# Edge aggregation of a graph layer: rank masks and running maxima moved into a PSUM bank

## What is computed

```
seg_sum  = segment_sum(edge_attr, src, 12500)
seg_max  = segment_max(edge_attr, src, 12500)        # 0 where a node has no edge
seg_mean = seg_sum / max(count, 1)
h   = relu(concat([seg_sum, seg_max, seg_mean, u]) @ W1 + b1)
out = x + h @ W2 + b2
```

## Time and profile before

| | |
|---|---|
| median of 3 runs | 4669.58 us (4665.87 to 4673.83) |
| the profiled execution | 4668.22 us, its span 4665.3 us |
| TensorE matmul busy | 3045.1 us, 65% of the span |
| VectorE busy | 2912.0 us, 62% |
| ScalarE busy | 1421.9 us, 30% |
| POOL busy | 3441.4 us, 74% |
| mean granted TensorE clock | 0.657 of full speed |

### The profile page before, as it was taken

How to read it: one execution, slowest core, us unless ns; L and a number is a source line. 1 busy time by engine, 2 the same in 40 slices (tenths; PEclk the granted TensorE clock), 3 DMA queues, 4 the chain that set the end, 5 groups by cost and what they waited for, 6 DMA issues and landing times.

```text
span 4665.3 us, 87454 instructions
## 1 busy us (share of the span) xinstructions
PE 3045.1 (65%) x18710; PEld 2270.5 (49%) x18710; DVE 2912.0 (62%) x11699; ACT 1421.9 (30%) x4649; POOL 3441.4 (74%) x3144
## 2 busy tenths in 40 slices
PE   5566667766666666666666777767766776677466
PEld 3455445544444444444444556555645555465345
DVE  6577557754555445555444777777757777577564
ACT  3322332233333333333333222222232222322133
POOL 5777778877777777777777788888877777788700
PEclk9977557855555555555555777777757777587666
DMA  7899863311111111111111333333213222133132
GB/s 288 325 354 338 323 219 103 89 24 25 26 26 25 25 25 25 26 26 25 25 25 50 93 92 92 92 92 92 69 53 85 77 76 76 55 95 108 38 113 77
DMA packets 410043, 454.46 MB, mean 97 GB/s; under 512 B 65002, under 2 KB 381460, under 8 KB 409620
## 3 DMA queue, kind: packets, MB, share of 16 engines
q1 hardware_dynamic: 309876, 401.37, 26.3%
q0 software_dynamic: 100000, 51.40, 4.6%
HBM read 221.50 MB, written 231.02 MB: 97 GB/s over the span
## 4 chain that ended last, share of the span: by engine, by line
POOL 69%; issue 22%; POOLq 3%; DMA 2%; DVE 2%; PE 1%; SPq 1%; ACT 0%; DVEq 0%; ACTq 0%
POOL sorted_rows L435 69%; POOLq L435 2%; DMA win<-sorted_rows 1%; DVE raised L786 1%; DVE raised L778 1%; DMA sorted_rows<-zeros 1%; POOLq L432 1%; DMA sorted_rows<-edges,position 0%; SPq L303 0%; POOLq L427 0%; POOLq L430 0%; PE misc_ps L577 0%; DMA edges<-in_edge_attr 0%; SPq L373 0%; DVE late L875 0%
## 5 line engine op out<-in xcount | busy, mean ns | idle before, releaser
L435 POOL DMA_INDIRECT sorted_rows<-edges,position x3125 | 3419.2, 1094 | 970.6 <-issue 969.6
L495 PE MATMUL place_ps<-start_sb,hot_block_t 98*128 98x128 bf16 x3125 | 889.7, 285 | 1227.5 <-DVE rank_f L719 1226.6
L606 ACT ACTIVATE start_sb<-start_ps 98x128 bf16<-98x128 f32 x3125 | 867.5, 278 | 1738.4 <-PE start_ps L491 844.4
L491 PE MATMUL start_ps<-hot_owner,hot_block 128*98 128x128 bf16 x3125 | 981.2, 314 | 149.5 <-ACT start_sb L606 107.2
L495 PEld LDWEIGHTS place_ps<-start_sb,hot_block_t 98*128 98x128 bf16 x3125 | 372.7, 119 | 1337.4 <-DVE rank_f L719 1317.7
L734 DVE SCALAR_TENSOR_TENSOR position<-rank_c,src_f 128x5 int32<-128x5 f32 x625 | 103.9, 166 | 1438.7 <-DMA sorted_rows<-edges,position 1429.0
L719 DVE CUSTOM_DVE_ANT_0 picked<-place_ps,hot_owner 128x128 bf16<-128x128 f32 x3125 | 885.8, 283 | 87.5 <-issue 72.1
L497 PE MATMUL place_ps<-hot_owner,earlier 128*128 128x128 bf16 x3125 | 898.3, 287 | 0.0
L491 PEld LDWEIGHTS start_ps<-hot_owner,hot_block 128*98 128x98 bf16 x3125 | 461.6, 148 | 627.5 <-ACT start_sb L606 621.7
L522 PE MATMUL misc_ps<-win,ident_f 128*128 128x224 f32 x2548 | 751.8, 462 | 0.0
L468 PE MATMUL same_ps<-hot_block_t 98*128 98x128 bf16 x3125 | 660.7, 290 | 86.0 <-DVE earlier L711 46.5
(11 more groups left out here) (76 smaller groups left out, 1367.1 us busy)
## 6 DMA issues: line engine op xcount, KB each, us to landing
sorted_rows<-zeros SPq DMA_DIRECT2D x110, 1568.0 KB, 25.8
win<-sorted_rows SPq DMA_DIRECT2D x56, 1344.0 KB
edges<-in_edge_attr SPq DMA_DIRECT2D x625, 80.0 KB
sorted_rows<-edges,position POOLq DMA_INDIRECT x3125
win<-sorted_rows SPq DMA_DIRECT2D x28, 1008.0 KB
win<-sorted_rows SPq DMA_DIRECT2D x14, 1680.0 KB
win<-sorted_rows SPq DMA_DIRECT2D x14, 1568.0 KB
win<-sorted_rows SPq DMA_DIRECT2D x14, 896.0 KB
```

Of the source, the lines that this page charges most:

```text
L435: nc.gpsimd.indirect_dma_start(out=rows[:, :], out_offset=bass.IndirectOffsetOnAxis(ap=position[:, t:t + 1], axis=0), in_=edges[:, k, j * ...
L491: nc.tensor.matmul(start_ps[0:BLOCKS, 0:P], hot_block[:, t, :], hot_owner[:, t, :], start=False, stop=False, skip_group_check=True).then_i ...
L495: nc.tensor.matmul(place_slot(j), hot_block_t[:, slot, j * P:(j + 1) * P], start_sb[:, j, :], start=True, stop=False)
L606: nc.scalar.activation(start_sb[:, j, :], start_ps[0:BLOCKS, 0:P], ACT.Copy)\
```

## The change

`peak_ps` is a PSUM bank of its own, 512 fp32 columns: `peak`, 448 columns, holds a running maximum of both halves of a pair, and `beyond`, 64 columns, holds the mask. The bank comes from `place_ps`, which shrinks from three banks to two; `PLACE_BANK` and `PLACE_USER` change accordingly, so tile 0 of a group now waits for the pick of tile 4 of the group before. `raised` has room for both halves, which is found by laying `paired` over `hot_block_t` and `earlier` (`lent`). Since 64 columns hold a mask of at most 9 planes, each half is masked and raised in two parts (`raise_part`). Half 0 is raised in group 0, half 1 in group 1; groups 2 and 3 take the maximum of both halves together, plane by plane, into `peak` (`take_ranks`), and `keep_peak` takes it into `run_max`. The last stage keeps halving `raised` (`take_max`), with the raise in two parts and the mask now behind the wait for the load.

```diff
+        peak_ps = ps("peak_ps", [P, BANK_COLS], FP32)
+        peak = peak_ps[:, 0:2 * COLS].rearrange("p (h n) -> p h n", h=2)
+        beyond = peak_ps[:, 2 * COLS:BANK_COLS]
...
-        PLACE_BANK = [0, 1, 0, 1, 2]
-        PLACE_USER = [3, 3, 2, 2, 5]
+        PLACE_BANK = [0, 1, 0, 1, 0]
+        PLACE_USER = [1, 3, 2, 2, 2]
...
+                def raise_part(s, h, col, r, a, z, steps):
+                    mask = beyond[:, 0:(z - a) * SLOTS].rearrange("p (r b) -> p r b", b=SLOTS)
+                    nc.vector.tensor_tensor(mask, left_t[...], iota_f[...], ALU.is_le).then_inc(unit_step, 1)
+                    dve.wait_ge(unit_step, steps + 1)
+                    return nc.vector.scalar_tensor_tensor(raised[:, h, a:z, :], mask, -FLT_MAX,
+                                                          win[:, h, a:z, :], ALU.mult, ALU.add)
+                def take_ranks(s, steps, a, z):
+                    for r in range(max(a, 1), z):
+                        prior = raised[:, :, 0, :] if r == 1 else peak
+                        if r > 1:
+                            dve.wait_ge(unit_step, steps + (r + 5))
+                        nc.vector.tensor_tensor(peak, raised[:, :, r, :], prior, ALU.max).then_inc(unit_step, 1)
+                def keep_peak(s, col, steps):
+                    dve.wait_ge(unit_step, steps + (depth[s] + 5))
+                    mine = run_max[:, bass.ds(col, 2 * SLOTS), :]
+                    nc.vector.tensor_tensor(mine, mine, peak, ALU.max).then_inc(unit_step, 1)
...
-                        if g in (0, 2):
-                            mark_beyond(of, col, r, steps + h * unit_steps[of])
-                            dve.wait_ge(win_loaded[h], p * 16 + 16)
-                            raise_half(of, h).then_inc(win_raised, 1)
-                        if g in (1, 3):
-                            dve.wait_ge(win_raised, p * 2 + (h + 3))
-                            take_max(of, col, steps + h * unit_steps[of])
+                        if g in (0, 1):
+                            dve.wait_ge(win_loaded[g], p * 16 + 16)
+                            if g == 1:
+                                dve.wait_ge(win_raised, p * 2 + 3)
+                            raise_half(of, g, col + g * SLOTS, r, steps + 3 * g)
+                        if g == 2:
+                            dve.wait_ge(win_raised, p * 2 + 4)
+                            take_ranks(of, steps, 0, half)
+                        if g == 3:
+                            take_ranks(of, steps, half, depth[of])
+                            keep_peak(of, col, steps)
```

More of the change, by code:

```diff
@@ L82, in build @@
     PAIRS = ROUNDS * sum(parts)
-    unit_steps = [2 + len(levels(d)) for d in depth]
-    step_base = [sum(2 * ROUNDS * parts[j] * unit_steps[j] for j in range(s)) for s in range(SEGS + 1)]
+    last_steps = 4 + len(levels(depth[LAST]))
+    pair_steps = [6 + d for d in depth[:LAST]] + [2 * last_steps]
+    step_base = [sum(ROUNDS * parts[j] * pair_steps[j] for j in range(s)) for s in range(SEGS + 1)]
     STEPS = step_base[SEGS]
@@ L774, in mark_beyond @@
                                             ALU.is_le).then_inc(unit_step, 1)
                     dve.wait_ge(unit_step, steps + 1)
-                def raise_half(s, h):
                     return nc.vector.scalar_tensor_tensor(
-                        raised[:, 0:depth[s], :].rearrange("p r (b f) -> p r b f", f=FEAT),
-                        beyond[:, 0:depth[s], :].unsqueeze(3).to_broadcast([P, depth[s], SLOTS, FEAT]), -FLT_MAX,
-                        win[:, h, 0:depth[s], :].rearrange("p r (b f) -> p r b f", f=FEAT), ALU.mult, ALU.add)
@@ L783, in take_max @@
-                def take_max(s, col, steps):
-                    left, done = depth[s], 1
-                    for folded, kept in levels(depth[s]):
-                        nc.vector.tensor_tensor(raised[:, 0:folded, :], raised[:, 0:folded, :],
-                                                raised[:, left - folded:left, :], ALU.max).then_inc(unit_step, 1)
+                        raised[:, h, a:z, :].rearrange("p r (b f) -> p r b f", f=FEAT),
+                        mask.unsqueeze(3).to_broadcast([P, z - a, SLOTS, FEAT]), -FLT_MAX,
```

54 lines of the change are left out of this document (33 added, 21 removed).

## The result

The changed kernel takes **4390.92 us** (median of 4 runs, 4387.55 to 4395.1), the kernel before 4670.3 us in the same comparison (4665.87 to 4673.83): a ratio of 0.9403, 95% interval 0.9386 to 0.9419. Forecast were 4375 us and a range of 4335 to 4465. The profiled execution took 4387.55 us, its span is 4385.8.

The account below looks back on a forecast made before the run. POOL's scatters were taken as the bound, held up by VectorE instructions with two SBUF inputs. 4668.2 - 319 + 12 (lag) + 12 (last stage) = 4373, with 1.4 for the median 4375 us; range 4335 to 4465.

Parts of the forecast that it names:

- Raises and maxima no longer hold POOL: Scatters beside a pair's reduction stop waiting for VectorE instructions with two SBUF inputs: -345.6 us at most, -319 after remaining holds.
- The one-hots: Stream instructions still with two SBUF inputs; hold scatters if VectorE stops waiting: +15 us, bounds 0 and 87.
- VectorE's work per pair: Masks, split raises and maxima in PSUM cost VectorE +1.5 us a pair at depth 12, +1.2 to +2.2 elsewhere.
- two passes in the bank: Rival: PSUM bank read and written in turn, each of 637 maxima 0.47 us dearer; about 4575 us, 5 in 100.
- the running maximum becomes the bound: Rival: the dependent row of maxima through one bank is slow, at 1.5 us each 4810 us; 4 in 100.
- the maxima still hold POOL: Rival: maxima with PSUM as second input still hold scatters, +73 us, 4448 us; 8 in 100.
- does not do what it says: Rival: the mask in PSUM frees nothing and the 345.6 us stay; 4682 us, 3 in 100.
- Both rules that were weighed: Skill rules: PSUM source 65 ns dearer, sum about 4390; raises at half rate from two SBUF inputs, sum 4363.
- What of it reaches POOL: VectorE's lag beyond its 23.6 us lead over POOL's scatters in the stream: +12 us, bounds 2 and 29.
- VectorE falls behind: Rival: maxima and raises each 0.1 us dearer, spill 54 us instead of 2; about 4425 us, 16 in 100.
- The last stage: Masks and a second raise part on the chain after the load: about 1.0 us for ten iterations, +12 us, bounds 5 and 20.
- DMA 0 and the placing banks 0: Neither busy DMA engines beside depth 8 nor fewer placing banks cost time; upper bounds 23 us and 0.3 us a group.

Follow-up runs that it names:

- all_in_sbuf: The changed kernel with the whole new bank, masks and running maximum, in SBUF instead of PSUM; order and split raises kept; 4511.79 us.
- maxima_only: The changed kernel with masks in SBUF and raises whole, as before the change; maxima plane by plane against the PSUM bank stay; 4552.07 us.
- whole_masks: last_as_before, with the stream's running maximum in SBUF, one whole PSUM mask for both halves and one raise a half; 4368.57 us.
- short_sums: The changed kernel with TensorE's sums beside the stream over only the first and last plane, so the result is not whole; 4368.06 us.
- last_as_before: The changed kernel with its last stage as before: one whole mask made before the wait for the load, one raise; 4386.39 us.
- banks_only: The kernel before, with only the placing products moved to two banks; 4674.93 us against 4669.89 in the same comparison.
- one_reduce: The changed kernel with the stream's chain of maxima replaced by one strided tensor_reduce per half; 4465.71 us.

## Why the prediction was right, and which terms were off

The forecast was the likeliest case with its sign and its main mechanism, 16 us short of the median. One of its own signs of being wrong came true all the same: POOL waits 39.9 us for `position`, and it had named 30; nor is POOL's idle time the 0.3 us a scatter that it had expected. By its own steps:

- **Raises and maxima no longer hold POOL:** right. Forecast -345.6 at most and -319 in the sum, measured -335.6. The masks in PSUM hold 0.2 us in all (forecast under 1), the first maxima 4.9 (forecast 56 x 0.155 = 9; with L less 0.17 the same formula gives 4.6). **The one-hots** were given +15, over a cost before that was taken as nothing; it was 15.7 us, and they took 22.3 - 15.7 = +6.6: the phase does wander, but VectorE still waits for POOL in most of the stream.
- **VectorE's work per pair:** right. The half raise is 1558 ns (1.56 forecast), the maximum 628 (0.62), a mask 211 (0.2); a mask written to SBUF takes 203 (all_in_sbuf), so the write to PSUM costs 8 ns. So "two passes in the bank" and "the running maximum becomes the bound" fell with these rows, "the maxima still hold POOL" with maxima_only, and "does not do what it says" with both. Both rules that were weighed are against the rows: 1558 ns for 1344 columns is what they take from two SBUF inputs too (1.56 us in all_in_sbuf). The Trainium skill ("VectorE: DVE Perf Modes", the errata section) had 65 ns more for a PSUM source, and by it the sum was 4390, next to the measured 4390.92; yet the maximum takes 628 ns from PSUM and 626 from SBUF (in whole_masks), so the time came out there by another way.
- **What of it reaches POOL:** the term that failed in size. I took +12, with bounds 2 and 29; measured +51.7. POOL's windows in the changed kernel, 11 chunks of depth 12 and 2 of depth 15 in which it follows VectorE:

```profile
2801.60:3187.40 385.80, 271.61 (x275) 0.79 0.35 103
4035.70:4110.10 74.40, 49.91 (x50) 0.82 0.25 71
```

  That is 35.1 us a chunk (forecast 33.5) and 37.2 (forecast 36.3). The step that failed is "its need is the stretch less its waits on scatters". The pair's own work is not the cause: masks, raises, maxima and the gaps before them take 15.3 us a chunk in these windows and took 13.8 before, the +1.5 of the forecast. Two other things make the 1.6. First, a `position` that no longer waits for a landing still starts 0.18 us behind `rank_c`, 0.90 us a chunk for five, where next to nothing (0.11) was left once the waits for landings were taken off: +0.8. Second, the 25 picks, with the gaps before them, take 6.25 us a chunk and took 5.37: +0.9. That second part is TensorE's: in a stretch of short_sums in which POOL follows VectorE the picks take 5.28 us again, and the 0.90 us stay:

```profile
2933.20:3171.50 238.30, 172.97 (x176) 0.52 0.36 106
```

  These are 7 chunks of 34.0 us, 1.0 less than in the changed kernel, and that at a lower clock. POOL's own chunk is 25 x (0.986 + 0.306) = 32.3 us at depth 12 and 32.5 at depth 15. With the measured need the forecast's own sum gives (35.1 - 32.3) x 21 = 59 us of lag against the lead of 23.6, 35 us spilled, and (37.2 - 32.5) x 7 = 33, 9 spilled; measured are 30.8 and 12.3. With 1.6 us more depth 14 spills too, some 9 us by the same sum, measured 7.7. The lead holds up; the need was too small.
- The rival "VectorE falls behind" had this mechanism, with 54 us in place of 2, and it came half true: its size of the spill, 54 against 51.7, was the right one. Its reason was not: maxima and raises are not 0.1 us dearer. Its time was not added up right either, since 54 us in place of the 12 make 4417 and not 4425; with 17 us fewer holds and 7 less in the last stage that comes to 4393, beside the measured 4391. What I had weighed as two cases was one case with a larger term.
- **The last stage:** +12 forecast, +5.4 measured. The split raise costs 0.7 us an iteration and not 1.0, 17.6 against 16.8 us, which makes 6.2 for the nine steps of that kind; the first four took 1.3 us together and the end of the network came 2.1 us earlier. last_as_before gives 9.1 back, so scatter between kernels of some 3 us is in both numbers.
- **DMA 0 and the placing banks 0:** right. Beside depth 8 VectorE's and POOL's times are as forecast though the DMA engines are at 1.01 of their time; banks_only has the same stream.

Sum of the terms: -335.6 + 51.7 + 5.4 = -278.5 measured, -295 forecast. Misses of -17, +40 and -7 us stand behind the 16 us; that the point was near is partly luck.

What stays open: why SP brings the edges late, by TensorE's sums or by the lag of the whole group; and what TensorE would take at an unchanged clock, since short_sums ran at a lower one.

## What to carry to other kernels

If GpSimd issues indirect DMAs, list the VectorE instructions with two SBUF inputs that run beside it: each one that is already running when a scatter starts costs POOL the rest of its length, less some 0.13 us. One input in PSUM ends that, at no price in VectorE's time; put the long ones there first, since a chain of short ones may cost almost nothing (the masks with the split raise are 240 us of the 280; of the 40 that the maxima add, plane by plane for levels, next to none is the running maximum's place in PSUM). When the bound moves, subtract from the second engine's stretch only the wait's excess over what it will still wait, and use the room in the bank to cut that engine's instructions: that was worth more than moving the last operand.

## What the runs showed of the hardware

- A scatter held by VectorE ends 0.85 us after the VectorE instruction, at 0.84 to 0.86 in 97 to 99 of 100 cases of the six kernels counted (676 of 679 in all_in_sbuf), whatever that instruction is: raise, level, maximum, bf16 one-hot.
- The instruction has to be under way when the scatter starts: begun 0.05 us or more before and still running 0.15 us after, it held 3939 of 3939; begun from 0.03 us before to 0.11 us after, 19 of 3428.
- With its mask in PSUM a raise at such times held 0 of 219 scatters in the changed kernel, a maximum with its second input in PSUM 0 of 220 in maxima_only, a reduction with its one input in SBUF 0 of 368 in one_reduce.
- A chain of short instructions and a queue of indirect DMAs fall in step. From the second scatter on, the hold is two steps of the chain less POOL's period: 0.035 us at a step of 0.659, 0.12 at 0.703, where the first scatter of a chain, which meets it by chance, is held 0.15 to 0.16 on average.
- A mask in PSUM costs VectorE what one in SBUF does, 2955 ns a whole raise in whole_masks against 2957 before. To write the small mask costs 8 ns more, 211 against 203.
- A `tensor_reduce` across a stride of 224 fp32 columns takes 1.70 ns a value, where a raise takes 1.04 a column.
